# A one-column memset between GpSimd's indirect transfers in the edge stage of a graph-network layer

## The reference, cut to what matters

```python
h   = relu(layernorm(x))                                   # x: 100000 nodes x 64
f_in = concat(h[src], h[dst], edge_attr)                   # 25000 edges x 192
r_in = concat(h[dst], h[src], edge_attr)
agg  = segment_sum(mlp2(f_in; W_f), dst) + segment_sum(mlp2(r_in; W_r), src)   # 100000 x 128
out  = x + h + mlp2(concat(agg, h); Wn)
```

## Time and profile before

| | us |
|---|---|
| median of 3 runs (lowest, highest) | 1618.86 (1618.42, 1619.26) |
| the profiled execution's own time | 1619.61 |
| its span in the trace | 1617.8 |
| GpSimd busy | 1111.7 (69% of the span) |
| TensorE matmul busy | 1288.9 (80%) |
| VectorE busy | 977.1 (60%) |
| ScalarE busy | 946.8 (59%) |
| mean granted TensorE clock | 0.853 of full speed |

### The profile page before, as it was taken

The page is one execution under the profiler, slowest core; times in us unless marked ns, Lnnn a source line. Parts: engine busy times, 40 slices in busy tenths (PEclk is TensorE's granted clock), DMA queues, the critical chain, the costliest instruction groups (busy, mean ns, idle before and its releaser), DMA issues.

```text
span 1617.8 us, 29085 instructions
## 1 busy us (share of the span) xinstructions
PE 1288.9 (80%) x7070; PEld 978.6 (60%) x7070; DVE 977.1 (60%) x2902; ACT 946.8 (59%) x2256; POOL 1111.7 (69%) x1003
## 2 busy tenths in 40 slices
PE   5899998457777787778788887777777756899998
PEld 4777776245556565656566665555556644666665
DVE  7999999436666666666666666666666641222222
ACT  5888888345555555545555555555554524677776
POOL 7888888888888888888888888888888861000000
PEclk9999999768888877877877778788887877999999
DMA  6899998435555555555555555555555547999997
GB/s 214 293 317 314 313 313 284 130 58 108 109 108 109 108 103 103 104 102 104 103 103 100 100 102 102 102 102 101 103 104 103 100 72 228 355 352 352 344 344 274
DMA packets 238374, 280.71 MB, mean 174 GB/s; under 512 B 53170, under 2 KB 155200, under 8 KB 238348
## 3 DMA queue, kind: packets, MB, share of 16 engines
q1 hardware_dynamic: 168408, 241.57, 45.0%
q0 software_dynamic: 68992, 38.59, 20.6%
q10 hardware_dynamic: 948, 0.30, 0.1%
HBM read 162.62 MB, written 117.72 MB: 173 GB/s over the span
## 4 chain that ended last, share of the span: by engine, by line
POOL 33%; issue 22%; DMA 15%; PE 4%; DVE 4%; ACT 1%; POOLq 0%; SPq 0%; another core or an unknown queue 0%; DVEq 0%; ACTq 0%
POOL table L532 27%; DMA out_x<-ncentred 12%; POOL got_odd L514 6%; DMA table<-to_send,scatter_at 2%; DVE ncentred L1137 2%; DVE same L979 1%; DMA same<-table 1%; PE bank L820 1%; PE bank L833 1%; PE bank L871 1%; PE bank L818 1%; PE bank L846 1%; PE bank L882 0%; SPq L391 0%; ACT nh L639 0%
## 5 line engine op out<-in xcount | busy, mean ns | idle before, releaser
L532 POOL DMA_INDIRECT table<-to_send,scatter_at x392 | 633.4, 1616 | 133.7 <-issue 119.2
L846 PEld LDWEIGHTS bank<-message,same 128*128 128x128 f32 x1960 | 271.1, 223 | 42.1 <-issue 39.2
L846 PE MATMUL bank<-message,same 128*128 128x128 f32 x1960 | 292.1, 314 | 2.7 <-DVE message L1010 2.7
L639 ACT ACTIVATE nh<-nx,all_sums,all_rstd 128x64 f32<-128x64 f32 x784 | 280.1, 433 | 0.0
L514 POOL DMA_INDIRECT got_even<-in_x,gather_first x196 | 212.0, 1082 | 40.4 <-issue 35.1
L775 PE MATMUL bank<-wn_h,nturned 128*128 128x256 f32 x784 | 197.4, 396 | 30.2 <-ACT nhidden L683 21.8
L514 POOL DMA_INDIRECT got_odd<-in_x,gather_at x180 | 179.9, 999 | 54.8 <-issue 54.2
L804 PE MATMUL bank<-ident,h_ends 128*128 128x128 f32 x196 | 54.1, 371 | 203.2 <-DVE h_ends L1019 200.8
L1004 DVE TENSOR_TENSOR scatter_at<-moved,ids 128x4 int32<-128x4 f32 x98 | 16.1, 165 | 303.3 <-DMA table<-to_send,scatter_at 303.3
L818 PE MATMUL bank<-turned,w_ends 128*128 128x256 f32 x392 | 167.0, 516 | 36.5 <-ACT turned_edge L609 36.5
L775 PEld LDWEIGHTS bank<-wn_h,nturned 128*128 128x128 f32 x784 | 143.7, 193 | 66.4 <-issue 37.8
(11 more groups left out here) (78 smaller groups left out, 1917.6 us busy)
## 6 DMA issues: line engine op xcount, KB each, us to landing
nx<-in_x SPq DMA_DIRECT2D x194, 256.0 KB
table<-nhidden SPq DMA_DIRECT2D x97, 512.0 KB
same<-table SPq DMA_DIRECT2D x97, 512.0 KB, 5.4
others<-numbers SPq DMA_DIRECT2D x196, 128.0 KB
out_x<-ncentred SPq DMA_DIRECT2D x97, 256.0 KB, 4.2
nx<-out_x SPq DMA_DIRECT2D x55, 256.0 KB, 4.7
out_x<-nh SPq DMA_DIRECT2D x31, 256.0 KB
table<-to_send,scatter_at POOLq DMA_INDIRECT x392
```

The lines of the kernel that those rows point to most:

```text
L532: pool.indirect_dma_start(table, bass.IndirectOffsetOnAxis(ap=scatter_at[s][:, k:k + 1], axis=0), to_send[s][:, k, :], None, compute_op=AL ...
L639: last = act.activation(nh[s][:, g, :], nx[place][:, g, :], ACT.Relu, bias=all_sums[:, at, g:g + 1].rearrange("p a g -> p (a g)"), scale=a ...
L846: last = pe.matmul(bank[6 + s][:, k * M:(k + 1) * M], same[s][:, o, k * P:(k + 1) * P], message[s][:, o, :], start=(o == k), stop=(o == KB ...
```

## The change

GpSimd gets a small buffer, `spacer` (128 partitions by 8 columns), that nothing reads. In each batch of the edge stage one column of it is set to zero before the second, third and fourth scatter (columns 0 to 2), and one before each of the two gathers (columns 3 and 4). No memset stands before the first scatter. The gathers of the first stage stay as they are. Each memset counts on a new semaphore, `s_spaced`, and before the first scatter of each batch but the very first GpSimd waits until all memsets of the batches before are done. In the hardware loop the value of this wait is 5 times the batch number.

```diff
+        spacer = sb("spacer", [P, 8])
...
+        s_spaced = sem("spacers_done")
...
-            def gather(to, numbers, landed, tiles=range(KB)):
+            def space(k):
+                pool.memset(spacer[:, k:k + 1], 0.0).then_inc(s_spaced, 1)
+
+            def gather(to, numbers, landed, tiles=range(KB), spaced=None):
                 for k in tiles:
+                    if spaced is not None:
+                        space(spaced + k % JT)
                     pool.indirect_dma_start(to[:, k * D:(k + 1) * D], None, x,
                                             bass.IndirectOffsetOnAxis(ap=numbers[:, k:k + 1], axis=0)
                                             ).then_inc(landed, 16)
+
+            def spaces(i, s):
+
+                n = 2 * i + s
+                return (KB - 1 + JT) * n if not isinstance(n, int) or n <= NB - 2 * LOOK else (
+                    (KB - 1) * n + JT * (NB - 2 * LOOK))
 
             def scatter(i, s):
                 pool.wait_ge(s_sat[s], i + 1)
...
+                if not first(i) or s == 1:
+                    pool.wait_ge(s_spaced, spaces(i, s))
                 pool.sem_inc(s_scatters_begun, 1)
                 for k in range(KB):
+                    if k > 0:
+                        space(k - 1)
                     pool.indirect_dma_start(table, bass.IndirectOffsetOnAxis(ap=scatter_at[s][:, k:k + 1], axis=0),
                                             to_send[s][:, k, :], None, compute_op=ALU.add).then_inc(s_added[s], 16)
...
-                gather(got_odd[place][:, 0, :], numbers, s_got[place], range(half * JT, (half + 1) * JT))
+                gather(got_odd[place][:, 0, :], numbers, s_got[place], range(half * JT, (half + 1) * JT), KB - 1)
```

## The result

| | before | changed |
|---|---|---|
| median of 15 runs, us | 1621.18 | 1624.10 |
| lowest to highest | 1618.42 to 1624.11 | 1621.01 to 1626.72 |
| ratio, 95% interval | | 1.0019, 1.0012 to 1.0026 |
| span of the profiled execution | 1617.8 | 1619.3 |

The changed kernel is slower by 2.9 us, 0.19%: a real loss, but one that sits just inside the 0.2% which the prediction called no change. The forecast was 1597. The level of the kernel before is 2.3 us higher over 15 runs than over the three shown ahead of the prediction, so every comparison here is made within one job.

The account below looks back on a forecast made before the run. GpSimd was taken to bound the edge stage. Gap -16.7, gathers -7.4 and wait +2 sum to -22.1 us, from 1619.6 to 1597.5, stated as 1597 us; forecast 1590 to 1606, range 1580 to 1625.

Parts of the forecast that it names:

- the term of the gap: Edge stage, idle time ahead of 478 spaced transfers: 0.27 us in place of 0.305, so -16.7 us.
- rival A: Gap of 0.30 is a floor that hides the memset; only gathers gain, 1613 us; chance 0.17.
- The second term: Edge-stage gathers: 0.96 us behind a memset in place of 1.02 and 0.98, in 92 batches, -7.4 us.
- The third term: Edge-stage scatters: durations unchanged by memsets between them, taken as nothing; bounds -7 and +11 us.
- the side on which I had put +11: Upper bound for scatters: memsets between them could keep them at the second's 1.61, +11 us.
- The fourth: New wait before a batch's first scatter: mostly hidden, 1.5 us plus 0.4 in the tail, +2 us.
- the slack that it would have eaten: Path from landed scatters to a batch's first scatter: 0.37 us spare, 0.27 used by shorter gathers, gaps and the wait.
- Rival D: Nothing to measure because small terms cancel, such as scatters at 1.61 against the gaps: 1619 us; chance 0.07.
- rival B: Memset comes on top of spaced gaps, slower once a gap exceeds 0.32 us: 1628 to 1661 us; chance 0.18.
- nothing becomes late: Other engines at -0.25 us a batch: VectorE keeps 3 us idle a batch, TensorE 2, so none turns late.
- the dispatch of tens of cycles: GpSimd software dispatch per memset: read naively an estimated 40 ns each, about +19 us in place of a gain.
- The contention of the port: VectorE two-port instructions hold GpSimd's write port pair, so a memset behind a comparison would stand still; no size given.

Follow-up runs that it names:

- e8: Kernel before, with the first stage's 208 memsets and their waits taken out: 1583.48 us, ratio 0.9775.
- e3: Changed kernel with no memset, the added wait kept on a count that is always met: 1622.50 us, ratio 1.0007.
- e2: Changed kernel with only the 184 memsets ahead of gathers and the wait, none between scatters: 1621.42 us, ratio 0.9999.
- e7: Kernel before, with the first stage's 208 memsets cut from 256 columns to one: 1584.98 us, ratio 0.9769.
- e1: Changed kernel with only the 294 memsets between scatters and the wait, none before gathers: 1625.35 us, ratio 1.0019 (interval 1.0007 to 1.0032).
- e9: Changed kernel with 16 columns in each of the 478 memsets in place of one: 1626.05 us, ratio 1.0025.
- e10: Changed kernel with two one-column memsets in each of the 478 places: 1624.21 us, ratio 1.0019.
- e11: Changed kernel without the first stage's memsets and their waits: 1842.87 us, ratio 1.1353.
- e12: Changed kernel with the first stage's memsets cut to one column, their waits kept: 1589.46 us, ratio 0.9804.

## Why the prediction was wrong

It failed in the term of the gap. I had written that a spaced gap would be 0.27 in place of 0.305 and that 478 of them give -16.7 us. The measured gap is 0.305, so the term is nothing. The working took the 0.49 us of the first stage and subtracted 255 columns, which gives the 0.284 of the line above; that arithmetic was right within 0.02 and described what the memset needs, not what the transfer needs. The profile of before held the hint: 0.30 is the same between all kinds of transfer, with three waits in it or with none. That was rival A's argument, and it had 0.17.

The second term, -7.4 us for the gathers, was wrong as well. I read 0.96 as an effect of the memset ahead of the gather. It is a gather's time deep in a run of gathers; e8 has 0.95 with no memset anywhere, and the changed kernel has 1.02 and 0.98 where before had them. Nothing had been held constant in that comparison but the kind of instruction, and rival A carried this error too: with its 1613 it was right about the gap and wrong about the time.

The third term, nothing for the scatters, was too low, by the side on which I had put +11. They rose by 4.7 us in sum between these two profiles, and the fourth of a batch by 13 ns. They did not go to the second scatter's 1.61, as the bound supposed, but rose by a smaller amount that has no row in the trace of before.

The fourth, +2 us for the wait, was not borne out: e3 gives 1 us, with an interval that holds nothing and 2 as well (0.9993 to 1.0022), and the gap ahead of the first scatter did not move. But the slack that it would have eaten was not shortened by the gathers either, so this term was never put to the test that I worked out for it.

With 0 for the gap, 0 for the gathers, 0 for the wait and +4.7 for the scatters the sum is 4.7 us over before. The measured difference is 2.9, with an interval of 1.9 to 4.2 (0.12% to 0.26% of 1621), and 5.6 in the edge stage of one profile. One profile each is not enough for the last microsecond. Five profiles without a memset ahead of scatters (before, e2, e3, e7, e8) have scatter sums of 633.1 to 634.3 us and edge stages of 1005.4 to 1006.8; five with short ones (the change, e1, e9, e10, e11) have 636.7 to 638.1 and 1009.2 to 1011.0. Their means differ by 3.8 and 4.3 us, 3.8 is also 294 times 13 ns, and it lies inside the interval of the runs.

The 1624.10 lies inside the range of 1580 to 1625, but that is luck: the range reached up to 1625 for the sake of the rivals, and neither they nor the forecast had what happened. Rival D, with 1619 and 0.07, is the nearest as a number; yet nothing large cancelled here. The gap and the gathers gave nothing, and the scatters cost a little. In rival B's threshold a slip stands: with the +2 for the wait it is 0.305 + 5.4/478 = 0.316 and not 0.32, which matters little beside the 0.284 to 0.305 in question.

What held: GpSimd paces the edge stage, other engines have room, and nothing becomes late behind the change. Of the rules, the dispatch of tens of cycles in the Trainium skill (GPSIMD Engine Reference, 2.1 Instruction dispatch) fits in size: a further memset of one column costs 0.027 us here, all its work included, about 32 cycles at the 1.2 GHz that the page gives. It is only that the first one or two lie under the floor, so neither a gain nor its 19 us came. The contention of the port (the Trainium skill, SBUF — State Buffer, Who interferes with whom) was not what lengthened the scatters behind one-column memsets. In the last batch VectorE runs nothing, and there the scatter with no memset ahead takes 1.55 and the three others 1.57, where before all four took 1.55 (the last row is the fourth of before):

```profile
1344.11 1.55 POOL L549 DMA_INDIRECT table<-to_send,scatter_at  x1 [2.69 <-issue]
1345.97 1.57 POOL L549 DMA_INDIRECT table<-to_send,scatter_at  x1 [0.19 <-issue]
1347.84 1.57 POOL L549 DMA_INDIRECT table<-to_send,scatter_at  x1 [0.19 <-issue]
```
```profile
1343.22 1.55 POOL L532 DMA_INDIRECT table<-to_send,scatter_at  x1 [0.31 <-issue]
```

What the memset does to the scatter behind it was not found out.

## What to carry to other kernels

Between two indirect transfers on GpSimd there was room for a small job: one memset of one column or of 16, or two of one column, cost at most 3 ns on the gap; beyond that a column cost 0.84 ns and a further memset 27. The room was not quite free: a scatter with a memset ahead of it took 6 to 14 ns longer. A gap that is the same whatever lies around it may be a floor, which filling it with less does not lower, and before subtracting from a longer pattern one should ask which of two limits the shorter one will meet. The larger gain lay in a place that the change did not touch: 208 memsets of 256 columns that paced the first stage's gathers held up the edge stage by 35 us, and cutting them to one column gave 2.3%.

## What the runs showed that I had not expected

A memset's row on GpSimd can begin inside the scatter ahead of it: 0.56 to 0.74 us before the scatter's end, for all 386 memsets behind scatters in the changed kernel. Behind a gather it begins within some 10 ns of the gather's end, in all 300 cases, however long the gather. Either way a one-column row closes 0.11 us behind the transfer. The Trainium skill (Perfetto Trace Analysis, DMA Instruction — SWDGE (GPSIMD)) says that only two of the engine's cores, DSPs 0 and 1, write the descriptors. The rows behind scatters would fit cores that go on to the memset early, the rows behind gathers do not show it; no run here looks at single cores, so the cause of the early rows is not shown. The row's length (605 ns in the mean) is in any case not a cost; only the distance between the ends and starts of transfers is.

The same gathers at nearly the same pace left the first stage whole in e8 and starved it in e11, with 56 GB/s in place of 311 for 257 us. One run was profiled; all six took 1835 to 1846 us. A kernel that takes out such pauses has to be measured in its final form, and of the two fast variants I would take e7, which keeps a wait between gathers; e12 is a second kernel in which that was sound.
